# Cross-attention with shared rest tiles: the leftover query rows of two batches in one tile

## The reference, cut to what matters

```python
# B, Q, KV, NH, HD, TOPK = 16, 100, 722, 16, 32, 32
q = _split_heads(layernorm(x) @ Wq.T + bq, B, Q)
k = _split_heads(ctx @ Wk.T + bk, B, KV)
v = _split_heads(ctx @ Wv.T + bv, B, KV)
scores = jnp.einsum('bhqd,bhkd->bhqk', q, k) / sqrt(HD)
top_scores, top_idx = jax.lax.top_k(scores, 32)
w = jax.nn.softmax(top_scores, axis=-1)
top_v = jnp.take_along_axis(v[:, :, None, :, :], top_idx[..., None], axis=3)
out = jnp.einsum('bhqk,bhqkd->bhqd', w, top_v)
x = x + out.reshape(B, Q, 512) @ Wo.T + bo
```

## Time and profile before

| What | before |
|---|---|
| median of 3 runs (lowest, highest) | 2241.64 us (2240.93, 2244.67) |
| the profiled execution's own time | 2236.97 us |
| its span in the profile | 2235.2 us |
| PE busy | 2002.9 us, 90% |
| DVE busy | 1884.8 us, 84% |
| ACT busy | 1323.6 us, 59% |
| POOL busy | 1282.8 us, 57% |

### The profile page before, as it was taken

The page is one execution under the profiler, slowest core; times in us unless marked ns, Lnnn a source line. Parts: engine busy times, 40 slices in busy tenths (PEclk is TensorE's granted clock), DMA queues, the critical chain, the costliest instruction groups (busy, mean ns, idle before and its releaser), DMA issues.

```text
span 2235.2 us, 50529 instructions
## 1 busy us (share of the span) xinstructions
PE 2002.9 (90%) x19824; PEld 1559.2 (70%) x19824; DVE 1884.8 (84%) x3511; ACT 1323.6 (59%) x2640; POOL 1282.8 (57%) x1560
## 2 busy tenths in 40 slices
PE   1899999999988899999899999999989989899966
PEld 1556665656563778787787777777878778777753
DVE  4757676767644699999999999999999999999994
ACT  4333333333322577777677777777777777777753
POOL 2556565647443356566656656666566665665642
PEclk9999999999988999999999999999999999999977
DMA  5000000000036100000001000010001000100000
GB/s 197 7 21 13 24 13 23 13 24 13 23 141 143 31 19 14 26 24 29 19 21 39 19 21 26 14 39 19 21 27 31 21 19 21 39 19 21 8 2 12
DMA packets 41497, 70.40 MB, mean 31 GB/s; under 512 B 4638, under 2 KB 21166, under 8 KB 41260
## 3 DMA queue, kind: packets, MB, share of 16 engines
q1 hardware_dynamic: 35868, 56.31, 8.2%
q0 software_dynamic: 3632, 7.58, 1.4%
q10 hardware_dynamic: 1760, 3.28, 0.5%
HBM read 60.54 MB, written 9.86 MB: 31 GB/s over the span
## 4 chain that ended last, share of the span: by engine, by line
PE 46%; ACT 11%; issue 6%; DVE 3%; POOL 2%; DMA 1%; ACTq 0%; POOLq 0%; another core or an unknown queue 0%; DVEq 0%
PE ca_pF L88 7%; PE ca_pF L89 6%; PE ca_pF L90 6%; PE ca_pT L1137 4%; PE ca_pO L1184 4%; PE ca_pS L88 3%; PE ca_pS L90 3%; PE ca_pS L89 3%; PE ca_pX L1239 3%; PE ca_pX L1203 2%; PE ca_pX L1230 2%; ACT ca_W L1291 2%; ACT ca_top L1294 2%; ACT ca_S L1308 2%; ACT ca_S L1301 1%
## 5 line engine op out<-in xcount | busy, mean ns | idle before, releaser
L1511 DVE MATCH_REPLACE8 ca_W<-ca_top,ca_W 128x722 f32<-128x722 f32 (+1 forms) x624 | 553.6, 894 | 0.0
L1500 DVE MAX8 ca_top<-ca_W 128x8 f32<-128x722 f32 (+1 forms) x624 | 537.1, 899 | 1.7
L982 POOL TENSOR_TENSOR ca_S<-ca_S,ca_W 128x722 f32<-128x722 f32 (+1 forms) x208 | 358.9, 1746 | 120.1 <-ACT ca_W L1291 120.1
L960 POOL TENSOR_TENSOR ca_KL<-ca_K,ca_KH 128x384 fp32r<-128x384 f32 (+1 forms) x128 | 122.6, 958 | 198.0 <-ACT ca_KH L1283 195.5
L88 PE MATMUL ca_pS<-ca_KH,ca_QH 128*128 128x362 f32 (+1 forms) x384 | 147.7, 385 | 90.5 <-ACT ca_S L1308 85.9
L1301 ACT ACTIVATE ca_S<-ca_S,ca_shift 128x722 f32<-128x722 f32 (+1 forms) x208 | 175.8, 891 | 67.0 <-POOL ca_shift L974 66.8
L1491 DVE MAX8 ca_top<-ca_S 128x8 f32<-128x722 f32 (+1 forms) x208 | 180.9, 901 | 35.9 <-ACT ca_S L1308 35.2
L1313 ACT ACTIVATE ca_PT<-ca_pT 128x768 f32<-128x768 f32 (+1 forms) x208 | 163.0, 784 | 67.1 <-PE ca_pT L1137 62.9
L317 POOL TENSOR_TENSOR sa_ss<-sa_ss,sa_minus_half 100x16 f32<-100x16 f32 x64 | 187.1, 2940 | 19.5 <-DVE sa_ss L475 19.5
L1291 ACT ACTIVATE ca_W<-ca_W,ca_shift 128x722 f32<-128x722 f32 (+1 forms) x208 | 186.7, 897 | 9.9 <-DVE ca_W L1511 9.9
L88 PE MATMUL ca_pF<-ca_cH,ca_WkH 128*128 128x338 f32 (+1 forms) x512 | 186.3, 364 | 6.4 <-ACT ca_K L1281 6.4
(11 more groups left out here) (224 smaller groups left out, 5167.7 us busy)
## 6 DMA issues: line engine op xcount, KB each, us to landing
ca_raw<-in_ctxT SPq DMA_DIRECT2D x32, 384.0 KB, 4.3
ca_raw<-in_ctxT SPq DMA_DIRECT2D x32, 338.0 KB, 3.0
sa_xin<-in_x SPq DMA_DIRECT2D x16, 200.0 KB
sa_xres<-in_x SPq DMA_DIRECT2D x16, 200.0 KB
x_scratch<-sa_x SPq DMA_DIRECT2D x16, 200.0 KB
x_scratch<-y_scratch POOLq DMA_DIRECT2D x16, 200.0 KB, 13.9
ca_xin<-x_scratch SPq DMA_DIRECT2D x16, 200.0 KB
ca_x<-x_scratch SPq DMA_DIRECT2D x16, 200.0 KB
```

The source lines that it names most:

```text
L982: pool.tensor_tensor(S[k][rows, :], S[k][rows, :], W[r][rows, :], ALU.subtract).then_inc(p_ready, 1)
L1500: n_of[t.i] = order.mark(dve.max(top[r][rows, 8 * k:8 * k + 8], W[r][rows, :]))
L1511: ins = dve.match_replace(W[r][rows, :], eight, W[r][rows, :], REMOVED)
```

## The change

The 64 rest rows of an even batch and the 64 of the next, odd batch share one tile of 128 rows. An odd batch has steps 0 to 5 only, so a pair of batches has 13 steps and 25 tiles in place of 14 and 26. For that:

- The odd batch's rest scores are made in the even batch's step 5 (`rest_score`, behind the FFN matmuls) and copied to rows 64 to 127 of the rest tile's `S` (`keep_second_rest`). VectorE's first MAX8 of that tile waits for both copies.
- The slices of an odd batch therefore follow `PAIR_PLAN`: slice 7 in step 4 moves ahead of the second transposes, and slice 10 moves from step 5 to step 4.
- In an odd batch the next batch's first tiles are scored in step 5, so its query is rounded a step earlier: `high_query`, `high_rest_query`, `query_low` and `rest_query_low` move to step 4. Step 6 of an odd batch keeps slice 11 and the copying out of the FFN.
- `rest_values` runs in step 1 of the odd batch with 96 small matmuls for both batches. In an even batch step 1 instead finishes two full tiles (tiles 10 and 11 of the odd batch), and `place_output` of group 3 falls in step 2.
- The second batch's rest output is multiplied in the odd batch's step 1 and put aside (`second_rest`); ScalarE copies it to `ctxT` in step 2 of the next even batch, ahead of the output projection.

```diff
+PAIR = 2 * 4 * Tile.REST
+    RUN = [(b, s) for b in range(B) for s in range(7 - b % 2)]
+    PLACE = [(b, t.i) for b, s in RUN for t in STEPS[s]]
...
     PLAN = [([12], [13]), ([], [0, 1]), ([2], [3]), ([4, 5], [6]), ([], [7, 8, 9]), ([10], []), ([], [11])]
+    PAIR_PLAN = [([12], [13]), ([], [0, 1]), ([2], [3]), ([4, 5], [6]), ([7], [8, 9, 10]), ([], []), ([], [11])]
...
+            def rest_score(tb, tp, before):
+                pe.wait_ge(q_lo, tb.count(5, 5))
+                pe.wait_ge(k_lo, tb.count(8, 8))
+                pe.wait_ge(s_ready, before)
+                for keys, cols in KEYS:
+                    for g in range(4):
+                        rows = slice(4 * REST * g, 4 * REST * g + 4 * REST)
+                        last = split3(pe, pS[0:4 * REST, cols], RH[:, rows], RL[:, rows],
+                                      KH[tp][:, g, keys], KL[tp][:, g, keys], g == 0, g == 3)
+                last.then_inc(s_mm, 1)
...
+                for p in (tp, 1 - tp):
+                    for g in range(4):
+                        at = 4 * REST * p + REST * g
+                        for k in range(KC):
+                            last = pe.matmul(pO[3 * DH:128, NUM + at:NUM + at + REST],
+                                             V[p][:, k, 128 * g + 3 * DH:128 * g + 128],
+                                             PT[0][:, k, at:at + REST], start=k == 0, stop=k == KC - 1)
...
+                    if s == 5 and tiles and not b.const % 2:
+                        rest_score(bn, 1 - par, scored(b, NT))
                     if len(old) > 1:
                         values(*old)
...
+            def keep_second_rest(tb, tp, t):
+                act.wait_ge(s_mm, scored(tb, NT + 1))
+                act.activation(S[slot(tb, t)][4 * REST:128, :], scores[0:4 * REST, :], ACT.Copy).then_inc(s_ready, 1)
...
                     if len(coming) > 1:
                         keep_scores(*coming[1])
+                    if s == 5 and tiles and not b.const % 2:
+                        keep_second_rest(*coming[0])
+                    if s == 4 and tiles and nxt and b.const % 2:
+                        high_query(bn, scored(b, NT - 1))
+                        high_rest_query(bn, scored(b, 0))
+                    if s == 2 and prev and not b.const % 2:
+                        act.wait_ge(ot_ready, b.count(GROUPS, -1))
+                        act.wait_ge(second_ready, b.const // 2)
+                        act.activation(ctxT[3 * DH:128, :, T - REST:T], chunks(second_rest, 4), ACT.Copy).then_inc(ot_ready, 1)
...
-                        dve.wait_ge(s_ready, tb.count(NT, t.i + 1))
-                        dve.max(top[r][rows, 0:8], S[slot(tb, t)][rows, :]).then_inc(peaked, 1)
+                        dve.wait_ge(s_ready, scored(tb, t.i + 1 + t.rest))
+                        dve.max(top[r][:, 0:8], S[slot(tb, t)][:, :]).then_inc(peaked, 1)
```

More of the change, by code:

```diff
@@ L853, in tiles_at, with of @@
         def tiles_at(s, b, par, tiles, prev, nxt):
[L855 to L874, removed]
+            if tiles and s == 6 and b.const % 2:
+                return [], [], [], [], []
+            at = RUN.index((b.const, s)) if tiles else (s - 7 if b.const < 0 else len(RUN) + s)
+            def of(n):
+                if not 0 <= n < len(RUN):
+                    return []
+                ob, os = RUN[n]
+                return [(At(ob), ob % 2, t) for t in STEPS[os]]
+            return of(at), of(at - 1), of(at - 2), of(at + 1), of(at - 3)
         def parts_done(b, t):
-            return b.count(PARTS, min(2 * (t.i - t.i % 2) + 4, PARTS))
+            return parts(b, min(2 * (t.i - t.i % 2) + 4, 25))
         def group_of(t):
@@ new lines, in score @@
+                if t.rest:
+                    rest_score(tb, tp, scored(tb, NT - 1))
+                    return
+                if t.i == 0:
+                    pe.wait_ge(q_lo, tb.count(5, 4))
+                if t.t == 0:
+                    pe.wait_ge(k_lo, tb.count(8, 5 + t.g))
+                need(pe, s_ready, scored(tb, t.i))
+                rows = slice(128 * t.t, 128 * t.t + 128)
+                for keys, cols in KEYS:
+                    last = split3(pe, pS[:, cols], QH[:, t.g, rows], QL[:, t.g, rows],
+                                  KH[tp][:, t.g, keys], KL[tp][:, t.g, keys], True, True)
@@ L1285, in exps_left @@
             def exps_left(tb, tp, t):
-                r, rows = ring(t, tp), slice(0, t.rows)
-                ob, oi = before(tb, t, RING)
-                act.wait_ge(picked, tb.count(NT, t.i + 1))
-                act.wait_ge(shift_ready, tb.count(NT, t.i + 1))
-                act.activation(W[r][rows, :], W[r][rows, :], ACT.Exp, bias=shift[rows, r:r + 1],
+                r = ring(tb, t)
+                act.wait_ge(picked, done(tb, t.i))
+                act.wait_ge(shift_ready, done(tb, t.i))
@@ L1302, in exps @@
                                scale=SCALE).then_inc(e_ready, 1)
             def keep_scores(tb, tp, t):
-                ob, oi = slot_before(tb, t)
-                need(act, pt_mm, ob.count(NT, oi + 1))
-                act.wait_ge(s_mm, tb.count(NT, t.i + 1))
-                act.activation(S[slot(tb, t)][0:t.rows, :], scores[0:t.rows, :], ACT.Copy).then_inc(s_ready, 1)
+                need(act, pt_mm, last_user(tb, t, slot)[0] + 1)
+                n = scored(tb, t.i + 1)
+                rows = slice(0, 4 * REST) if t.rest else slice(0, 128)
@@ L1498, in body @@
                                 else:
                                     order.after(n_of[t.i])
-                                n_of[t.i] = order.mark(dve.max(top[r][rows, 8 * k:8 * k + 8], W[r][rows, :]))
+                                n_of[t.i] = order.mark(dve.max(top[r][:, 8 * k:8 * k + 8], W[r][:, :]))
                         for tb, tp, t in cur:
-                            r, rows = ring(t, tp), slice(0, t.rows)
-                            eight = top[r][rows, 8 * k:8 * k + 8]
+                            r = ring(tb, t)
@@ L1504, in body @@
+                            eight = top[r][:, 8 * k:8 * k + 8]
                             if k == 0:
-                                ob, oi = before(tb, t, RING)
-                                need(dve, p_ready, ob.count(NT, oi + 1))
-                                dve.wait_ge(peaked, tb.count(NT, t.i + 1))
-                                dve.match_replace(W[r][rows, :], eight, S[slot(tb, t)][rows, :], REMOVED).then_inc(removed, 1)
+                                need(dve, p_ready, last_user(tb, t, ring)[0] + 1)
+                                dve.wait_ge(peaked, done(tb, t.i))
+                                dve.match_replace(W[r][:, :], eight, S[slot(tb, t)][:, :], REMOVED).then_inc(removed, 1)
```

250 lines of the change are left out of this document (131 added, 119 removed).

## The result

| | before | changed |
|---|---|---|
| median | 2241.28 us (4 runs) | 2326.43 us (4 runs, 2319.45 to 2327.55) |
| ratio, 95% interval | 1 | 1.0379 [1.0361, 1.0396] |
| span in the profile | 2235.2 us | 2324.1 us |

The change costs 85 us by the medians. The prediction added 44.5 to the profiled execution of before, and its 2282 is 41 above the median; 2326 lies above the range's top of 2304. First the page of the changed kernel: the busy table, and the shares of the chain that ended last.

A forecast was written before the change was run, and what follows sets the result against it. TensorE's ring with ScalarE was taken as the bound. New waits of 13.3 less 7.3 gave +6.0 us a pair, 42 for seven pairs; with the ends +39.5, clock +5, on 2236.97: 2282, range 2246 to 2304.

The forecast's parts named there:

- the ends: First and last batches: batch 0 +4 for the rest score's wait, the last batch -6.5 for its removed step.
- The clock: Slow-clock stretches on TensorE behind long waits: 0 to 2 a pair, 0 to 21 us, counted as +5.
- 1: slice 9 behind the query's copies: Odd step 4: slice 9 waits longer for ScalarE's copy of slice 7, now behind the query's copies: +1.5 us a pair.
- 2: score of tile 0 waits for `QL`: Odd step 5: TensorE's score of the next batch's tile 0 waits for GpSimd's `QL`: 4.5 us a pair.
- 3: rest score waits for `RL`: Even step 5: the odd batch's rest score waits for `RL`: 3.9 us a pair.
- 4, and the waits for `pS` filled or gone (1.90, 1.95, 0.36): Even step 1's second score waits +1.6 us a pair; waits of 1.90, 1.95 and 0.36 in other steps go.
- 1.24 twice a pair: Wait behind the transposes in both steps 5 gets work in between and goes: 2.48 us a pair saved.
- 5: output projection waits for `ctxT`: Even step 2: the output projection waits for ScalarE's copy of `second_rest`: +1.8 us a pair.
- worse than the sum: Rival, chance 0.15: two slow-clock stretches a pair and a `QL` wait of 6 us, 10.5 a pair: +71, 2308.
- The even and odd batch: Even batch about 98 us, odd 88; VectorE's waits for score tiles rise from 2 to 10 to 16 a pair.
- VectorE is the bound: Rival, chance 0.12: VectorE sets the pace, so the removed tile gives 7.7 a pair, 62 us in all: time 2180.
- the new waits only fill slack: Rival, chance 0.10: new waits fall into old slack, -1.8 to +1 us a pair: time 2225 to 2250.

The follow-up runs named there:

- experiment 7: Changed kernel with unused 128-column products (37, 27, 18, 18, 16) that end inside five TensorE waits a pair: 2289.39 us, ratio 1.0221.
- experiment 4: Kernel before the change, with 24 and 22 unused 128-column products in its waits of 2.12 and 1.90: 2229.09 us, ratio 0.9947.
- experiment 6: Changed kernel with slice 7 back behind the second score of even step 4: 2357.42 us, ratio 1.0519.
- experiment 5: Changed kernel with tile 0's score behind the FFN and slice 10 in odd step 5, and `RL` made ahead of `QL` in even step 5: 2240.29 us.
- experiment 1: Changed kernel with the score of tile 0 moved behind the FFN and slice 10 in odd step 5: 2273.61 us, ratio 1.0138.
- experiment 2: Changed kernel with GpSimd making `RL` ahead of `QL` in even step 5: 2278.88 us, ratio 1.0168.
- experiment 9: ScalarE's `second_rest` copy moved right behind the first score's copy, against experiment 5's kernel with fillers in three waits (2226.84 us): 2216.02 us, ratio 0.9888.
- experiment 10: Experiment 9's kernel with the query rounded behind the copies of key slices 8 to 10 in odd step 4: 2208.78 us, ratio 0.9849.
- the repaired one: The kernel of experiment 5, both repairs in the changed kernel: 2240.29 us; with unused products in three waits 2226.84 us.

## Why the prediction was wrong

The direction and the mechanism were right: VectorE's relief isn't collected, and TensorE's ring gets new waits at the query's low halves. **The step that failed first is the term "The clock": "0 to 2 a pair, so 0 to 21 us. I count +5".** The kind of cost was right and its size was not: the runs showed about 25 us (experiment 7 less experiment 4, 37 - 12), above the top of the term. That alone would make 2302, so the rest of the error lies in waits that the sum hadn't and in the ends. Over the six pairs, TensorE's waits from the rows above, and the prediction's terms times six:

| term, six pairs | predicted | measured |
|---|---|---|
| 1: slice 9 behind the query's copies | +9.0 | 8.0 - 4.3 = +3.7 |
| 2: score of tile 0 waits for `QL` | 27.0 | 25.4 |
| 3: rest score waits for `RL` | 23.4 | 19.7 |
| 4, and the waits for `pS` filled or gone (1.90, 1.95, 0.36) | -15.7 | 45.8 - 55.8 = -10.0 |
| 1.24 twice a pair | -14.9 | 1.6 - 14.9 = -13.3 |
| 5: output projection waits for `ctxT` | 10.8 | 9.0 |
| slice 7 waits for `ca_cL` | none | 9.5 |
| waits for `PT` and `NR` | none | 6.6 |
| TensorE's idle time, all | +39.6 | +48.7 |
| TensorE's busy time | -3.6 | +20.5 |

The rows on waits add to 50.6; small waits that the view doesn't list make the difference to 48.7. The 1.24 that the prediction put down to a ScalarE copy has `issue` for its releaser in the earlier trace rows; the copy of `PT` did end just ahead of it, at 1468.29.

**The clock.** The busy time is off by 24.1 us in the six pairs, where 5 were allowed for the whole program. I had seen one slow stretch behind a wait of 1.90 and none behind the 2.12 of the same batch, and took the latter for the rule. The next, even batch showed otherwise: behind its 2.12 the clock was 0.57 to 0.59, in all six pairs. Reading both batches would have given 13 stretches for 24 waits, two a pair. At the price from experiment 6, 2.2 to 2.6 us and not 1.5, the 12 more of the changed kernel are 26 to 31 us. Experiments 5, 6 and 7 show the term from three sides. The rival "worse than the sum" had this mechanism, at 1.5 us a stretch: 2308, still 18 too low.

**The waits' sum** is off by 9.1 us: the two rows that were missed are 16.1, and terms 1, 2, 3 and 5 came out smaller. I costed slice 7 by TensorE's time and didn't ask when GpSimd has its operand ready. Terms 2, 3 and 5, the core of the argument, stand within 17% each, and experiments 1, 2 and 9 each removed one of them and had its price back, 1 and 2 with the clock's on top. The size of term 1 was an overestimate by 5 us, and experiment 10 shows that what it blames, ScalarE's order, only hands the wait on.

**The ends.** Batch 0 takes 96.8 us from one query projection to the next, before 86.9: +9.9 and not +4. With no older batch's work ahead, TensorE comes to the rest score much earlier and waits longest of all:

```profile
PE ca_pS L88 <- POOL ca_RL L1042: 8.9, 1, 8.9
```

I had taken the steady batch's 3.9 for it. With `RL` made first (experiment 2) this wait is 4.2 us and batch 0 takes 92.6. From the end of the six pairs to the end, batches 13 to 15, the changed kernel takes 287.4 us, before 278.6: +8.8, where the sum had +6.0 - 6.5 = -0.5. The even batches from 2 on went from 89.9 to 101.5, most of them; if batch 14 is like these (an estimate), +11.6, batch 13 (+1.9) and batch 15 leave -4.7 for the last, not -6.5. Together: six pairs +33.2 over the 36 predicted, batch 0 +5.9, the last batches +9.3, the start of the loop +1.0 later, less the 5 counted for the clock, is 44.4, the whole error by the profiles (88.9 less 44.5). Of it the clock has about 19 in the six pairs (24.1 less the 5), the single largest part. These are sums of the two profiled executions. On the medians the change cost 85.2, not 88.9, and 4.3 us of the error come from starting at the profiled execution, 2236.97, and not at the median.

**The even and odd batch.** Predicted 98 and 88, measured up to 101.6 and 93.1. VectorE waits 125.2/6 = 20.9 us a pair, not 10 to 16, since it waits for what TensorE loses to the clock too: with the fillers of experiment 7 it is (57.3 + 37.2)/6 = 15.8. Its loss at the rest tile, 11 us, is just above the 5 to 10.

**The rivals.** That VectorE is the bound falls twice: with 4% less work in each pair the kernel got slower, and in experiment 1 its longest wait stayed while 53 us went. By the Trainium skill's rule (Perfetto Trace Analysis, "Identifying the Most-Contended Engine") VectorE would have been optimized first; here the busy times pointed at the wrong ring and the chain at the right one. Even in experiment 10 VectorE has (1062.6 - 1028.8)/6 = 5.6 us a pair to spare. That the new waits only fill slack falls with experiment 5: the two are worth 86 us.

## What to carry to other kernels

A wait on a busy TensorE can cost more than its length. Read the granted clock behind every wait of the steady part, not behind one or two, and put the stretches into the sum by their number and price (here 25 of 32 waits, 2.2 to 2.6 us each). Before an engine's work is cut because it is busy 98% of the time, follow which other ring turns at the same speed: what the cut moves is paid for there, and the order on a helper engine (which of two small results GpSimd makes first, 47 us here) can be worth more than the cut. For each operand of a piece that is moved ahead ask when its last writer is through, and ask it of the first batch of a pipeline too, where less work stands ahead.

## What the runs showed of the hardware

- The same wait of 2.12 us in odd step 4 left the granted clock at 1.00 in the kernel before and was followed by 0.62 in the changed one, in the pair shown; over the six pairs it had a slow stretch behind it once before and four times in the changed kernel. So a wait's length doesn't tell alone whether the clock falls; what else decides was not tried. The Trainium skill (TensorE: Matmul & The Clock Gate, "HAM oscillation — how this bites in real kernels") tells of a kernel that pays the slow clock anew behind each wait for a DMA. These traces agree, for waits on ScalarE and GpSimd, with the addition that 7 of 32 were followed by none.
- One more wait of 2.12 us a pair (experiment 6) raised the slow stretches in the six pairs by ten, from 25 of 32 waits to 35 of 37: waits that had none behind them before now have one.
- Products of 128 columns that nobody uses, kept inside the waits, paid in each kernel: 12 us before, 37 in the changed one, 13 in the repaired one. Where they overran the waits, at 0.11 us each, 32 us of the 37 were lost again.
